# A two-layer adaLN kernel: the expert weight of the first mixture of experts as a square root, spread by DMA

## The chip, the cores and the metric

The kernel runs on one core of one Trainium2 chip. The time is the device time of one execution in microseconds (us). TensorE (PE in the profile) multiplies matrices into the eight banks of PSUM; VectorE (DVE) and ScalarE (ACT) work elementwise on tiles of 128 partitions; SyncE (SP) issues most of the transfers, which run on 16 DMA engines; GpSimd (POOL) is nearly idle here.

## The reference, cut to what matters

Two layers, each of attention and a feed-forward part, over 2048 tokens of width 128. The change is in the first feed-forward part alone, a mixture of 64 experts of which each token uses 8, plus a shared expert:

```
logits = xf @ router_w.T ; scores = sigmoid(logits)
choose 4 of 8 groups, then 8 of 64 experts (by scores + bias)
tw  = scores of the chosen / (their sum + 1e-20) * 2.5          # the combine weight, >= 0
out = sum over experts e:  ( relu(x @ up[e])^2 * tw[:, e] ) @ down[e]     up 128x64, down 64x128
```

Since tw is not negative, relu(u)^2 * tw equals (relu(u) * sqrt(tw))^2.

## The kernel before, in words

Everything is hand-scheduled: each engine has its own program, and semaphores join them. Tokens lie in four chunks of 512 (`NC` = 4). Two experts form a pair, so that one tile has 128 hidden rows; there are 32 pairs, and pair by chunk gives 128 **units**. Weights of four pairs come in one load (`load0`, two slots), which the diff calls slot 0 and slot 1; a loop iteration on every engine has `MU` = 32 units (8 pairs, two loads), and there are four iterations. ScalarE (`high0`) and VectorE (`low0`) split each load into a high and a low fp32r part, in two pieces each, between units; PE waits for these parts (`w0_lo`) before the first unit that uses them.

One unit is, before the change:

- PE, `look0`, three units ahead: three fp32r matmuls (`three`: high by high, high by low, low by high) give the up projection in PSUM bank k % 2; one bf16 matmul with the constant `sel` (a 96-row selector over three bf16 parts of the weights) spreads the combine weights of the pair's two experts over 2 x 64 partitions, in bank 2 + k % 2 (line 839).
- ACT: Relu out of PSUM (`relu0`, L1222), Square (`sq_unit`, L1226), and for three units in four the high fp32r part of the product (`high_unit`, L1231).
- DVE: the product of the spread weight in PSUM and the square (`prod_unit`, L1677), for every fourth unit the high part (L1684), and the fp32r difference (`low_unit`, L1688).
- PE, `sum0`: three fp32r matmuls of the down projection, accumulated in banks 4 to 7.

Ahead of the loop stands the routing on DVE, lines 1580 to 1635, whose last result `b1` (a 128x16x64 tile) is the combine weight; lines 1645 to 1654 split it into three bf16 parts, PE transposes them (L812, L814), and ACT and DVE copy them out of PSUM (L1217, L1704). SP has nothing to issue in the loop but the weight loads (L545, L547). The second layer's mixture of experts already spreads its own weights in the other way: it stores them in DRAM (L618) and reads one row of 2048 back into all 128 partitions (L622).

Of the kernel before, what the change touches and what calls it, by code (L numbers as in the profile page):

```python
# [10 lines left out]
F32 = mybir.dt.float32  # L11
# [6 lines left out]
P = 128  # L18
# [16 lines left out]
EH = E0 // 2  # L35
NCB = 3 * EH
# [67 lines left out]
def adaln_two_layers(nc, A, out):  # L104
    ctx = ExitStack()
    with ctx:
# [105 lines left out]
        comb3 = take([2, NT, 3, EH], BF16)  # L212
        combT = take([2, T], BF16)
        sel = take([NPAIR // 2, P], BF16)
# [4 lines left out]
        relu = take([NBUF, CW])  # L219
        hid = take([2, CW])  # L220
        yT = take([T])
# [53 lines left out]

        cw_dram = nc.dram_tensor("expert_weights", [E1, T], F32).ap()
# [61 lines left out]
        rt_ready = sem("rt_ready")  # L338
        yg_ready = sem("yg_ready")
# [10 lines left out]
        comb_ready = sem("comb_ready")  # L350
        comb_tr = sem("comb_tr")
        comb_T = sem("comb_T")
        comb_TL = sem("comb_TL")
        moe_up = sem("moe_up")
        moe_cb = sem("moe_cb")
        moe_relu = sem("moe_relu")
# [3 lines left out]
        moe_hi_own = sem("moe_hi_own")  # L360
# [81 lines left out]

        def comb_bank(c):
            return 2 - 2 * (c % 2)
# [46 lines left out]
        def _(sp):  # L491
# [73 lines left out]
            sp.dma_start(sel, A["sel"].rearrange("p (n f) -> p n f", f=P)).then_inc(ld_sel, 16)  # L565
# [76 lines left out]
        def _(pool):  # L642
# [9 lines left out]
            pool.wait_ge(vzero, 2)  # L652
            pool.wait_ge(x2_ready, NC)
# [8 lines left out]
        def _(pe):  # L662
# [117 lines left out]
            pe.wait_ge(ld_sel, 48)  # L780
# [22 lines left out]
            pe.wait_ge(ld_c, 16 * 11)  # L803
            for c in range(NC):
                pe.wait_ge(comb_ready, 2)
                if c >= 2:
                    pe.wait_ge(comb_T, c - 1)
                    pe.wait_ge(comb_TL, c - 1)
                b = comb_bank(c)
                pc = ps[:, b:b + 2, :].bitcast(BF16)  # L810
                for k, t in enumerate(tiles(c)):
                    nc.tensor.transpose(pc[0:NCB, 0, k * P:(k + 1) * P],  # L812
                                        comb3[:, 0, t].rearrange("p s e -> p (s e)"), identb[:, :])
                    last = nc.tensor.transpose(pc[0:NCB, 1, k * P:(k + 1) * P],  # L814
                                               comb3[:, 1, t].rearrange("p s e -> p (s e)"), identb[:, :])
                last.then_inc(comb_tr, 1)
            pe.wait_ge(comb_T, NC)
# [1154 lines left out]
```

## Time and profile before

| | us |
|---|---|
| median of 3 runs | 1312.22 |
| the runs | 1310.79, 2832.59, 1312.22 |
| the profiled execution, span from first to last instruction | 1317.5 |
| PE busy | 1166.7 |
| DVE busy | 1046.4 |
| ACT busy | 776.6 |
| bytes read from and written to DRAM | 30.85 MB, 3.08 MB |

For the profiled execution the page gives its span and no other time; the span is 5.3 us above the median. Busy times overlap between engines. Matmuls are pipelined, so a matmul's duration is longer than the distance to the next one. The granted TensorE clock is a share of full speed: 1.00 is 2.4 GHz and 0.50 is 1.2 GHz. The DMA share is the mean busy share of the 16 DMA engines; it is computed from the packets, which may overlap a little, so that a full set of engines reads 0.97 to 1.06.

### The profile page before, as it was taken

Reading aid. Unit: us, or ns where it says so; the run is one execution under the profiler, and the core shown is the slowest. Engines: PE = TensorE matmul, PEld = TensorE weight load, DVE = VectorE, ACT = ScalarE, POOL = GpSimd, SP = SyncE. Lnnn points to the kernel's source line nnn. Section 1 sums busy time; section 2 is a strip of 40 time slices with the busy share of each in tenths; the row PEclk is TensorE's granted clock in tenths of the full one; section 3 lists DMA queues with packets and bytes.
Section 4 is the critical chain, followed back from the end, with each engine's and each line's share of the span. In section 5 each row is a group of like instructions: output and inputs, shape, how many; then the busy total and the mean of one; then the engine's idle time right before and its main releaser. Section 6 shows DMA issues by size and latency. Waiting matters only on the chain.

```text
span 1317.5 us, 17710 instructions
## 1 busy us (share of the span) xinstructions
PE 1166.7 (89%) x6249; PEld 680.9 (52%) x6249; DVE 1046.4 (79%) x2018; ACT 776.6 (59%) x1151; POOL 43.9 (3%) x45
## 2 busy tenths in 40 slices
PE   3888647999999855779999999999998799999998
PEld 2333333666666512345444443443332688888886
DVE  4699998788888883879899889888851688888885
ACT  1635414899999710135555656566676566666664
POOL 0000020000000040140000000000000000000000
PEclk9898767899999956589999999999999699999999
DMA  5000000000000214551000000000000121111001
GB/s 161 0 0 1 0 24 17 16 17 16 18 14 1 78 35 79 72 78 16 2 2 2 1 1 2 1 1 1 1 1 1 45 102 56 56 56 56 0 1 33
DMA packets 38169, 35.02 MB, mean 27 GB/s; under 512 B 15162, under 2 KB 33530, under 8 KB 36810
## 3 DMA queue, kind: packets, MB, share of 16 engines
q1 hardware_dynamic: 36082, 31.12, 9.0%
q0 software_dynamic: 2016, 2.96, 1.7%
q8 instruction: 44, 0.72, 0.2%
q14 instruction: 27, 0.22, 0.1%
HBM read 30.85 MB, written 3.08 MB: 26 GB/s over the span
## 4 chain that ended last, share of the span: by engine, by line
PE 61%; DVE 26%; ACT 6%; issue 3%; DMA 3%; SPq 1%; DVEq 0%; ACTq 0%
PE ps L822 10%; PE ps L823 10%; PE ps L824 10%; PE ps L983 9%; DVE arena_a L1766 7%; PE ps L927 7%; PE ps L971 6%; DVE arena_b L1472 3%; DVE mv L1377 2%; PE ps L839 1%; ACT arena_b L1222 1%; DMA arena_a<-q_parts 1%; PE ps L693 1%; DMA arena_a<-arena_a 1%; DVE xn L1384 1%
## 5 line engine op out<-in xcount | busy, mean ns | idle before, releaser
L1766 DVE TENSOR_REDUCE arena_a<-ps 128x1 f32<-128x512 f32 (+3 forms) x560 | 344.4, 668 | 73.2 <-PE ps L931 46.3
L1289 ACT ACTIVATE arena_b<-ps 128x1024 f32<-128x1024 f32 (+3 forms) x320 | 274.0, 894 | 191.8 <-PE ps L971 169.6
L822 PE MATMUL ps<-parts 128*128 128x512 f32 x640 | 273.2, 427 | 7.1 <-DVE parts L1688 4.2
L823 PE MATMUL ps<-parts 128*128 128x512 f32 x640 | 251.5, 393 | 0.0
L824 PE MATMUL ps<-parts 128*128 128x512 f32 x640 | 251.2, 392 | 0.0
L927 PE MATMUL ps<-arena_b,arena_a 128*128 128x512 bf16 (+3 forms) x576 | 190.4, 354 | 6.3 <-DVE arena_a L1766 4.9
L971 PE MATMUL ps<-arena_a,arena_b 128*128 128x512 bf16 (+3 forms) x576 | 163.2, 348 | 0.7 <-ACT arena_b L1289 0.3
L983 PE MATMUL ps<-arena_b 128*32 128x512 f32 (+3 forms) x1280 | 151.1, 544 | 2.5 <-DVE arena_b L1754 2.2
L822 PEld LDWEIGHTS ps<-parts 128*128 128x128 f32 x640 | 122.0, 191 | 36.8 <-DVE parts L1688 9.7
L824 PEld LDWEIGHTS ps<-parts 128*128 128x128 f32 x640 | 121.0, 189 | 26.4
L823 PEld LDWEIGHTS ps<-parts 128*128 128x128 f32 x640 | 121.4, 190 | 22.4
L1867 DVE TENSOR_TENSOR arena_b<-ps,arena_b 128x512 f32<-128x512 f32 x128 | 88.3, 690 | 55.4 <-PE ps L824 51.6
L927 PEld LDWEIGHTS ps<-arena_b,arena_a 128*128 128x128 bf16 x576 | 52.8, 99 | 143.0 <-DVE arena_a L1766 119.0
L1312 ACT ACTIVATE arena_b<-ps 128x512 f32<-128x512 f32 x128 | 76.6, 599 | 84.5 <-PE ps L824 84.0
L1677 DVE TENSOR_TENSOR arena_b<-ps,arena_b 128x512 f32<-128x512 f32 x128 | 88.1, 689 | 35.2 <-ACT arena_b L1226 34.8
L1688 DVE TENSOR_TENSOR parts<-arena_b,parts 128x512 fp32r<-128x512 f32 x128 | 87.6, 685 | 1.2
L1872 DVE TENSOR_TENSOR parts<-arena_b,parts 128x512 fp32r<-128x512 f32 x128 | 87.3, 682 | 0.1
L1226 ACT ACTIVATE arena_b<-arena_b 128x512 f32<-128x512 f32 x128 | 80.7, 631 | 3.6
L1222 ACT ACTIVATE arena_b<-ps 128x512 f32<-128x512 f32 x128 | 74.9, 585 | 9.2 <-PE ps L824 9.1
L1316 ACT ACTIVATE parts<-arena_b 128x512 fp32r<-128x512 f32 x128 | 79.9, 624 | 0.4 <-DVE arena_b L1867 0.4
L971 PEld LDWEIGHTS ps<-arena_a,arena_b 128*128 128x128 bf16 x576 | 53.3, 99 | 35.0 <-ACT arena_b L1289 13.4
L930 PE MATMUL ps<-arena_b,arena_a 128*128 128x128 bf16 x256 | 53.8, 236 | 12.0 <-DMA arena_a<-q_parts 12.0
(274 smaller groups left out, 1445.3 us busy)
## 6 DMA issues: line engine op xcount, KB each, us to landing
arena_b<-expert_weights SPq DMA_DIRECT2D x7, 1024.0 KB, 6.7
arena_a<-q_parts SPq DMA_DIRECT2D x18, 128.0 KB
arena_a<-q_parts POOLq DMA_DIRECT2D x18, 128.0 KB, 5.9
wslot<-in_L_ffn_up_w SPq DMA_DIRECT2D x8, 256.0 KB, 3.1
wslot<-in_L_ffn_down_w SPq DMA_DIRECT2D x8, 256.0 KB, 3.3
wslot<-in_L_ffn_w_gate SPq DMA_DIRECT2D x8, 256.0 KB, 2.9
wslot<-in_L_ffn_w_up SPq DMA_DIRECT2D x8, 256.0 KB, 3.4
wslot<-in_L_ffn_w_down SPq DMA_DIRECT2D x8, 256.0 KB, 3.8
```

Source lines behind the costliest of these rows:

```text
L822: mm(bank, w(0), x(0), start=start, stop=False)
L823: mm(bank, w(0), x(1), start=False, stop=False)
L824: return mm(bank, w(1), x(0), start=False, stop=stop)
L927: last = mm(b[:, at_:at_ + full], q, kst[:, g, u * CW:u * CW + full], start=True, stop=True)
L971: last = mm(ps[:, 2 + i, full:CW], k, q[:, full:CW], start=True, stop=True)
L983: last = mm(ps[32 * i:32 * i + 32, 6, off:CW], vaug[:, j, g, :], probs[:, s % 2, i, off:CW], start=(j == 0), stop=(j == TPC * c + TPC - 1) ...
L1222: a(relu[:, k % NBUF, :], ps[:, k % 2, :], ACT.Relu).then_inc(moe_relu, 1)
L1289: a(probs[:, s % 2, 2 * pair:2 * pair + 2, off:CW], ps[:, 2 + 2 * pair:4 + 2 * pair, off:CW], ACT.Exp, scale=scale).then_inc(p2_exp, 1)
L1677: v.tensor_tensor(prod0[:, k % NBUF, :], ps[:, 2 + k % 2, :], sq0[:, k % NBUF, :], ALU.mult)\
L1688: v.tensor_tensor(hid0[:, k % NBUF, 1, :], prod0[:, k % NBUF, :], hid0[:, k % NBUF, 0, :].bitcast(F32), ALU.subtract).then_inc(moe_lo, 1)
L1766: v.tensor_reduce(mx[:, n % 2, i:i + fit, t % TPC, u], b[:, 0:fit * w].rearrange("p (h k) -> p h k", k=w), AX_X, ALU.max)\
L1867: v.tensor_tensor(prod1[:, k % NBUF, :], ps[:, 2 + k % 2, :], silg[:, k % 2, :], ALU.mult)\
```

## The change

Three things are changed. First, the routing ends with the square root of the combine weight: ACT takes the root, DVE corrects it by one Newton step, PE transposes the result in fp32 and ACT copies it to `scT` (64 rows by 2048). Second, SP stores `scT` in DRAM (`root_weights`) and loads it back for each pair, spread over the partitions: two rows of 2048, each to 64 partitions, into one of four buffers `cbw`. The spreading matmul goes, with `sel`. Third, the unit is another: DVE forms max(up, 0) * root straight from PSUM, two units ahead; ACT squares that twice, once to fp32 (`sq0`) and once to fp32r (`hid0` high part), and DVE takes the difference of the two. The up projection now has four PSUM banks.

```diff
+            for c in range(NC):
+                sp.wait_ge(comb_T, c + 1)
+                sp.dma_start(sc_dram[:, chunk(c)], scT[0:E0, chunk(c)]).then_inc(st_sc, 16)
+            sp.wait_ge(st_sc, 16 * NC)
+            def load_cb(buf, pair):
+                sp.dma_start(cbw[:, buf, :], sc_dram[bass.ds(2 * pair, 2), :].unsqueeze(1).broadcast_to([2, I0, T]))\
+                  .then_inc(ld_cb[buf], 16)
+            for pair in range(NCBUF):
+                load_cb(pair, pair)
+            for pair in range(NCBUF, 2 * GP):
+                sp.wait_ge(moe_prod, NC * (pair - NCBUF + 1))
+                load_cb(pair % NCBUF, pair)
             with sp.Fori(1, N_IT0) as it:
                 for slot in range(2):
                     sp.wait_ge(w0_lo, it * 4 + (2 * slot - 2))
                     load0(slot, it * 2 + slot)
+                    for k in range(GP):
+                        pair = slot * GP + k
+                        sp.wait_ge(moe_prod, it * MU + NC * (pair - NCBUF + 1))
+                        load_cb(pair % NCBUF, it * (2 * GP) + pair)
...
@@ PE, look0
-                if n0 is not None:
-                    pe.wait_ge(moe_relu, n0 + (k - 1))
-                three(ps[:, k % 2, :], lambda i: up0(slot, i, pair % GP), lambda i: hs0[:, i, chunk(c)],
+                if n0 is None:
+                    pe.wait_ge(comb_T, k + 1)
+                else:
+                    pe.wait_ge(moe_prod, n0 + (k - 3))
+                three(ps[:, k % 4, :], lambda i: up0(slot, i, pair % GP), lambda i: hs0[:, i, chunk(c)],
                       True, True).then_inc(moe_up, 1)
-                w = sel[0:NCB, bass.ds(base + pair % GP, 1), :].rearrange("p a f -> p (a f)")
-                mm(ps[:, 2 + k % 2, :], w, combT[0:NCB, slot, chunk(c)], start=True, stop=True).then_inc(moe_cb, 1)
...
@@ ACT
-            def relu0(n0, k):
...
-            def sq_unit(n0, k):
...
-            def high_unit(n0, k):
+            act.wait_ge(comb_ready, 1)
+            a(b2, b1, ACT.Sqrt).then_inc(rt0_ready, 1)
+                a(scT[0:E0, chunk(c)], ps[0:E0, c, :], ACT.Copy).then_inc(comb_T, 1)
+            def square_unit(n0, k):
                 act.wait_ge(moe_prod, n0 + (k + 1))
-                a(hid0[:, k % NBUF, 0, :], prod0[:, k % NBUF, :], ACT.Copy).then_inc(moe_hi, 1)
+                a(sq0[:, k % NBUF, :], prod0[:, k % NBUF, :], ACT.Square).then_inc(moe_sq, 1)
+                a(hid0[:, k % NBUF, 0, :], prod0[:, k % NBUF, :], ACT.Square).then_inc(moe_hi, 1)
+            def units0(n0, loads, last_iteration):
                 for k in range(MU):
+                    square_unit(n0, k)
                     half, u = k // HALF, k % HALF
                     if u in (4, 6) and not (last_iteration and half):
                         high0((half + 1) % 2, u // 2 - 2, loads * 16 + (32 if half == 0 else 64))
...
@@ DVE
+            dve.wait_ge(rt0_ready, 1)
+            chain(v.tensor_scalar(msk, b2, 1e-18, None, ALU.max))
+            chain(v.reciprocal(sfc, msk))
+            chain(v.scalar_tensor_tensor(sfc, b1, 0.5, sfc, ALU.mult, ALU.mult))
+            v.scalar_tensor_tensor(b1, b2, 0.5, sfc, ALU.mult, ALU.add).then_inc(root_ready, 1)
...
+            def prod_unit(n0, it, k):
+                pair, c = k // NC, k % NC
+                if c == 0:
+                    dve.wait_ge(ld_cb[pair % NCBUF], it * (16 * 2 * GP // NCBUF) + 16 * (pair // NCBUF + 1))
+                dve.wait_ge(moe_up, n0 + (k + 1))
+                v.scalar_tensor_tensor(prod0[:, k % NBUF, :], ps[:, k % 4, :], 0.0, cbw[:, pair % NCBUF, chunk(c)],
+                                       ALU.max, ALU.mult).then_inc(moe_prod, 1)
+            def low_unit(n0, k):
                 dve.wait_ge(moe_sq, n0 + (k + 1))
...
+                dve.wait_ge(moe_hi, n0 + (k + 1))
+                v.tensor_tensor(hid0[:, k % NBUF, 1, :], sq0[:, k % NBUF, :],
                                 hid0[:, k % NBUF, 0, :].bitcast(F32), ALU.subtract).then_inc(moe_lo, 1)
```

How the instructions now stand. First SP's queue from the routing to the end of the loop; in the order `arena_a<-root_weights` is the load of one pair's roots and `wslot<-in_L_ffn_up_w` and `..._down_w` one load of weights. Before:

```order
L562 DMA arena_b<-in_L_ffn_shared_up_w 128x256 [waits x1_ready]
L563 DMA arena_b<-in_L_ffn_shared_down_w 128x2x128
L565 DMA arena_a<-in_sel 128x2048
L567 UNCONDITIONAL_BRANCH
L567 ISA
L545 ISA [waits w0_lo]
L545 DMA wslot<-in_L_ffn_up_w 128x8x64
L547 ISA
L547 DMA wslot<-in_L_ffn_down_w 128x4x128
```

and after the change:

```order
L565 DMA root_weights<-arena_b 64x512 [waits comb_T] x4
L570 DMA arena_a<-root_weights 128x1x2048 [waits st_sc]
L570 DMA arena_a<-root_weights 128x1x2048 x3
L570 DMA arena_a<-root_weights 128x1x2048 [waits moe_prod] x4
L578 UNCONDITIONAL_BRANCH
L578 ISA
L542 ISA [waits w0_lo]
L542 DMA wslot<-in_L_ffn_up_w 128x8x64
L544 ISA
L544 DMA wslot<-in_L_ffn_down_w 128x4x128
L584 ISA
L570 ISA [waits moe_prod]
```

Each load of weights in the loop now stands behind a load of roots that waits for DVE's products, where before it waited for `w0_lo` alone.

Second, ACT just inside the loop. Before, the unit was three instructions with three waits:

```order
L1222 ACTIVATE arena_b<-ps 128x512 [waits moe_up]
L1226 ACTIVATE arena_b<-arena_b 128x512 [waits moe_relu]
L1231 ACTIVATE parts<-arena_b 128x512 [waits moe_prod]
L1221 REGISTER_ALU
L1222 ACTIVATE arena_b<-ps 128x512 [waits moe_up]
```

and after the change it is two with one wait; this stretch is units 4 to 6, where the first piece of a new load of weights (`high0`, L1213) comes between:

```order
L1235 ACTIVATE arena_b<-arena_b 128x512 [waits moe_prod]
L1236 ACTIVATE parts<-arena_b 128x512
L1212 ISA
L1213 ACTIVATE parts<-wslot 128x512 [waits ld_w0_1]
L1234 REGISTER_ALU
L1235 ACTIVATE arena_b<-arena_b 128x512 [waits moe_prod]
L1236 ACTIVATE parts<-arena_b 128x512
```

ACT's squares of unit 5 stand behind its wait for the load of weights, as the Square of unit 5 did before.

## Rows read from the trace of the kernel before

**Rows 1.** Stretches of the loop: length; busy of each engine (instructions); clock; DMA share; GB/s.

```profile
235.00:450.00 215.00, 211.19 (x886) 145.84 (x885) 180.91 (x299) 202.32 (x366) 0.00 (x0) 0.99 0.05 13
300.00:440.00 140.00, 137.58 (x584) 95.62 (x582) 119.03 (x197) 132.24 (x240) 0.00 (x0) 1.00 0.05 11
```

**Rows 2.** Groups by line, 300 to 450: busy, mean ns of one | idle before, releaser.

```profile
L839 PE MATMUL ps<-arena_a 96*128 96x512 bf16 x89 | 34.8, 391 | 0.0
...
L1677 DVE TENSOR_TENSOR arena_b<-ps,arena_b 128x512 f32<-128x512 f32 x90 | 62.0, 689 | 21.9 <-ACT arena_b L1226 21.6
L1688 DVE TENSOR_TENSOR parts<-arena_b,parts 128x512 fp32r<-128x512 f32 x89 | 60.9, 685 | 0.7
L1226 ACT ACTIVATE arena_b<-arena_b 128x512 f32<-128x512 f32 x90 | 56.8, 631 | 2.5
```

**Rows 3.** Timeline, end of the routing to the loop: start, length, engine, line.

```profile
222.93 1.22 DVE L1635 SCALAR_TENSOR_TENSOR arena_a<-arena_a,arena_b 128x1024 f32<-128x1024 f32 x1
...
233.02 0.77 PE L822 MATMUL ps<-parts 128*128 128x512 f32 x1 [0.73 <-DVE arena_a L1704]
...
237.55 1.29 DVE L1677 TENSOR_TENSOR arena_b<-ps,arena_b 128x512 f32<-128x512 f32 x2 [4.80 <-ACT arena_b L1226]
```

**Rows 4.** Groups by line and shape, DVE from 20 to 240, ACT over the span.

```profile
L1486 DVE RECIPROCAL arena_b<-arena_a 128x512 f32<-128x512 f32 x4 | 13.4, 3348 | 2.2 <-ACT arena_a L1157 2.1
L1441 DVE TENSOR_SCALAR arena_b<-arena_a 128x2048 f32<-128x2048 f32 x4 | 4.9, 1228 | 0.1
L1480 DVE SCALAR_TENSOR_TENSOR arena_a<-ps,arena_a 128x512 f32<-128x512 f32 x4 | 2.8, 691 | 0.1
L1477 DVE TENSOR_SCALAR arena_a<-arena_a 128x512 f32<-128x512 f32 x4 | 1.6, 406 | 0.0
```

**Rows 5.** The same view, ACT.

```profile
L1152 ACT ACTIVATE arena_b<-arena_b 128x2048 f32<-128x2048 f32 x8 | 15.3, 1911 | 38.1 <-DVE arena_b L1472 38.1
...
L1214 ACT ACTIVATE arena_b<-arena_b 128x512 f32<-128x512 f32 x8 | 5.0, 630 | 0.3
```

**Rows 6.** Timeline of SP: the store and the first spread load of layer two.

```profile
1046.28 0.30 SPq L618 DMA_DIRECT2D expert_weights<-arena_b  x1
1048.72 0.37 SPq L622 DMA_DIRECT2D arena_b<-expert_weights  x1
```

**Rows 7.** Page, DMA issues: count, KB each, us to landing.

```profile
arena_b<-expert_weights SPq DMA_DIRECT2D x7, 1024.0 KB, 6.7
```

**Rows 8.** Stretches in which loads of 128 rows run (columns as in rows 1).

```profile
10.00:12.00 2.00, 2.00 (x12) 2.00 (x11) 0.00 (x0) 0.00 (x0) 0.00 (x0) 1.00 1.06 400
1056.50:1057.50 1.00, 1.00 (x6) 0.84 (x5) 0.59 (x1) 0.41 (x1) 0.00 (x0) 1.00 0.97 393
1049.80:1058.70 8.90, 8.90 (x39) 7.30 (x39) 6.01 (x10) 6.08 (x11) 0.00 (x0) 0.98 0.90 327
```

**Rows 9.** Stretches in which only loads of 8 rows run (L482, L485).

```profile
514.00:516.00 2.00, 0.00 (x0) 0.00 (x0) 0.00 (x0) 0.00 (x0) 0.00 (x0) 0.50 0.56 62
516.00:518.00 2.00, 0.00 (x0) 0.00 (x0) 0.00 (x0) 0.00 (x0) 0.00 (x0) 0.50 0.58 61
518.00:520.00 2.00, 0.00 (x0) 0.00 (x0) 0.00 (x0) 0.00 (x0) 0.00 (x0) 0.50 0.59 68
```

**Rows 10.** A stretch with one packet, and 20 us with one load of weights.

```profile
273.50:273.82 0.32, 0.32 (x3) 0.25 (x3) 0.20 (x1) 0.32 (x2) 0.00 (x0) 1.00 0.06 26
300.00:320.00 20.00, 19.52 (x84) 13.37 (x83) 16.99 (x29) 18.92 (x35) 0.00 (x0) 1.00 0.10 26
```

**Rows 11.** Timeline, the last unit of the loop.

```profile
449.93 0.69 DVE L1677 TENSOR_TENSOR arena_b<-ps,arena_b 128x512 f32<-128x512 f32 x1 [0.38 <-ACT arena_b L1226]
...
452.90 0.39 PE L824 MATMUL ps<-parts 128*128 128x512 f32 x1
```

**Rows 12.** Page, share of the span on the chain that ended last, by line.

```profile
PE ps L822 10%; PE ps L823 10%; PE ps L824 10%; PE ps L983 9%; DVE arena_a L1766 7%; PE ps L927 7%; PE ps L971 6%; DVE arena_b L1472 3%; DVE mv L1377 2%; PE ps L839 1%; ACT arena_b L1222 1%; DMA arena_a<-q_parts 1%; PE ps L693 1%; DMA arena_a<-arena_a 1%; DVE xn L1384 1%
```

More of the change, by code:

```diff
@@ L34 @@
 NSH = ISH // P
[L35 to L36 removed]
+NCBUF = 4
 LOOK = 3
@@ L210, in adaln_two_layers @@
         b2 = take([NT, E0])
-        comb3 = take([2, NT, 3, EH], BF16)
-        combT = take([2, T], BF16)
-        sel = take([NPAIR // 2, P], BF16)
+        at[0] = PW1 - NCBUF * T
+        cbw = take([NCBUF, T])
         gsm = take([7, NT * NG0])
@@ L218, in adaln_two_layers @@
         wsh = take([2, ISH])
-        relu = take([NBUF, CW])
+        relu = take([2, CW])
         hid = take([2, CW])
+        scT = take([T])
         yT = take([T])
@@ L274, in adaln_two_layers @@
         obuf = take([NT, D])
+        sc_dram = nc.dram_tensor("root_weights", [E0, T], F32).ap()
         cw_dram = nc.dram_tensor("expert_weights", [E1, T], F32).ap()
@@ L350, in adaln_two_layers @@
         comb_ready = sem("comb_ready")
+        root_ready = sem("root_ready")
         comb_tr = sem("comb_tr")
         comb_T = sem("comb_T")
-        comb_TL = sem("comb_TL")
+        st_sc = sem("st_sc")
+        ld_cb = [sem(f"ld_cb{b}") for b in range(NCBUF)]
         moe_up = sem("moe_up")
-        moe_cb = sem("moe_cb")
-        moe_relu = sem("moe_relu")
         moe_sq = sem("moe_sq")
@@ L824, in three, with look0 @@
                 return mm(bank, w(1), x(0), start=False, stop=stop)
-            def look0(base, k, n0, loads):
+            def look0(k, n0, loads):
                 pair, c = k // NC, k % NC
@@ L849, in _ @@
             for k in range(LOOK):
-                look0(0, k, 0 if k >= 2 else None, 2)
-            with pe.Fori(0, N_IT0 - 1) as it:
+                look0(k, None, 2)
+            look0(LOOK, None, 2)
+            sum0(0, 0, False)
+            for k in range(1, MU):
+                if k + LOOK < MU:
+                    look0(k + LOOK, 0, 4)
+                else:
+                    look0(k + LOOK - MU, MU, 6)
+                sum0(0, k, False)
+            with pe.Fori(1, N_IT0 - 1) as it:
                 for k in range(MU):
                     if k + LOOK < MU:
-                        look0(it * GP, k + LOOK, it * MU, it * 4 + 4)
+                        look0(k + LOOK, it * MU, it * 4 + 4)
                     else:
-                        look0(it * GP + GP, k + LOOK - MU, it * MU + MU, it * 4 + 6)
+                        look0(k + LOOK - MU, it * MU + MU, it * 4 + 6)
                     sum0(it * MU, k, False)
@@ L1634, in _ @@
             chain(v.reciprocal(wsum[:, 2, :], wsum[:, 1, :]))
[L1635 to L1654 removed]
+            v.scalar_tensor_tensor(b1, b2, 2.5, wsum[:, 2, :].unsqueeze(2).broadcast_to([P, NT, E0]),
+                                   ALU.mult, ALU.mult).then_inc(comb_ready, 1)
+            dve.wait_ge(rt0_ready, 1)
[3 more added lines that the diff above has]
+            v.scalar_tensor_tensor(b1, b2, 0.5, sfc, ALU.mult, ALU.add).then_inc(root_ready, 1)
             dve.wait_ge(ld_c, 16 * 11)
@@ L1939, in _constants @@
     sin = np.sin(ang).astype(f32).T[d // 2] * np.where(d % 2 == 0, -1.0, 1.0).astype(f32)[:, None]
-    sel = np.zeros((P, NPAIR // 2, P), f32)
-    for n in range(NPAIR // 2):
-        for j in range(2):
-            for m in range(3):
-                sel[m * EH + 2 * n + j, n, j * I0:(j + 1) * I0] = 1.0
     return {
```

99 lines of the change are left out of this document (17 added, 82 removed).

## The prediction, made before the changed kernel was run

> **What bounds the kernel now.** I read the chain of waits first, then the loop's own stretches, then the groups by line, and last the DMA views, since the change moves work from TensorE to the DMA engines. On the chain the matmuls of `three` hold 30% of the span and the spreading matmul 1% [rows 12]. The first layer's loop runs from about 233 to 453 us [rows 3, 11]. In it TensorE is busy 137.58 of 140 us at full clock with 584 matmuls [rows 1], that is 0.236 us for each, and seven to a unit make 1.65 us; ScalarE is busy 132.24 and VectorE 119.03 of the 140 [rows 1]. So TensorE bounds, with ScalarE right behind it: VectorE's idle time of 21.9 us is spent on ScalarE's Square [rows 2]. The DMA engines do almost nothing there: share 0.05, 11 GB/s [rows 1]. Over the whole loop that is 886 recorded matmuls in 215 us [rows 1], or 1.7 us for a unit.
>
> **What the change takes from the unit.** One matmul in seven goes: 0.236 us for each of 128 units, 30 us at most. ScalarE goes from a Relu, a Square and three quarters of a copy to two Squares, of 0.631 us [rows 2] or less: 1.26 us for a unit. VectorE's product becomes one instruction that reads PSUM and a tile; its nearest row, L1480, takes 0.691 us [rows 4], as the old product did with 0.689 [rows 2]; the difference stays at 0.685; the fourth part of a copy goes. So about 1.38 us of VectorE, 1.26 of ScalarE and 6 x 0.236 = 1.42 of TensorE. By compute alone a unit would take 1.42 us, TensorE still ahead. The waits between engines are covered by the two units that VectorE works ahead.
>
> **What it adds to the unit.** The roots now arrive by DMA: each pair needs 1 MiB in `cbw`, 32 MiB in all, more than the whole kernel reads now. A pair's four units take 4 x 1.42 = 5.7 us, so the load must land at 184 GB/s or the loop waits for it. Here lies the decision, and two groups bear on it. Loads with 128 rows keep all 16 engines busy: share 0.97 to 1.06 at 393 and 400 GB/s [rows 8], some 25 GB/s for each engine. Loads whose pattern has only 8 rows outermost, issued by the same SP queue and with many waiting at once, stop at a share of 0.56 to 0.59 [rows 9], half of the full set; 61 to 68 GB/s, since their packets are small. Half the engines for 8 rows means that the engines used are as many as the outermost dimension allows. The new load's source is [2 rows, 64 repeats, 2048 elements]. Its outermost dimension is 2, while the tile written has 128 partitions. The second layer's load, whose source is [128 repeats, 2048], is not like it: it has 128 outermost. If the smaller side decides, two engines carry a pair, 0.5 MiB each.
>
> No row has a load with unlike outer dimensions on its two sides, so the 8-row loads leave open which side counts. The Trainium skill ("DMA: Bandwidth & Descriptors", Why a DMA increments its semaphore by 16 and not by 1) says that a transfer runs on the largest number of engines up to 16 that divides the slowest dimension of both sides; its Rules for kernel authors warn of just such a leading dimension of few copies. By that rule the number here is 2; this trace agrees for 8 and shows nothing for 2 against 128. I take two engines.
>
> **The price of a pair on two engines.** One packet running alone gives 26 GB/s on one engine (share 0.06 is one sixteenth) [rows 10]. With all engines full it is 393/(16 x 0.97) = 25.3 GB/s, and over the second layer's loads 327/(16 x 0.90) = 22.7 [rows 8]. 524,288 bytes on each engine then take 20.2, 20.7 or 23.1 us. I take 20.2, since two engines alone are nearer to the lone packet than to the full set; 23.1 is the upper bound. Below, nothing in the trace is faster. The skill's page gives 27 GiB/s per engine (Specifications); by that alone a pair would take an estimated 18.1 us and the total would be 67 us lower. No run here shows it.
>
> 20.2 us is 3.5 times what the pair's units need, so all of the compute hides behind the loads, and the gain of 30 us is worth nothing.
>
> **The sum, on the profiled execution.**
> - The combine weight is ready at 222.93 + 1.22 = 224.15 us [rows 3].
> - ScalarE's root of 1024 elements: between 0.630 for 512 and 1.911 for 2048 [rows 5], 1.06 us. Its table load (order: ahead of the wait) is hidden in ScalarE's idle time behind the routing.
> - VectorE: maximum, 0.69 us (0.406 for 512, 1.228 for 2048, both in rows 4); reciprocal, twice 3.348 [rows 4] = 6.7; two combining instructions like L1635, 1.22 each [rows 3]. 9.8 us, and about 235.1 us with the root.
> - Sixteen transposes and four copies of about 0.6 us, pipelined as before: 3.3 us, 238.4.
> - Store and wait as in layer two: from the store's issue to the load's, 2.44 us [rows 6]: 241. The first byte some 2 us later: 243. (By now the old loop had begun ten us before, at 233 [rows 3]; the split of lines 1645 to 1654 and its transposes and copies, all on the path, are what it replaces.)
> - 32 pairs one after the other, 32 x 20.2 = 646 us: 889.
> - The six loads of weights inside the loop run through the same two engines: share 0.10 of 20 us [rows 10], 2 us each, 12 us: 901.
> - After the last pair has landed, its four units: the last one from product to last matmul 452.90 + 0.39 - 449.93 = 3.4 us [rows 11], three before it at 1.42 us each, or twice that if TensorE sits at half clock, together 8 to 12 us. I take 9: 910.
>
> The old loop ended at 453.3, so 457 us are added: a span of 1774 us. The median of the runs stood 5.3 us below the profiled span, so **1769 us**.
>
> Two engines must never run dry for this sum. Four buffers allow it: a pair's load is issued when the products of the pair four before are done, so two or three are always queued. The new queue order costs something else: a load of weights stands behind the loads of roots. ScalarE asks for it at units 4 and 6 of each half, and then stands for nearly two pairs, 40 us, with VectorE stopped two or three units later. But in that time two further pairs' loads can be issued and the twelve or so resident units take only 16 to 30 us to catch up. I cost this at nothing; it is covered by the loads themselves. If that cover is gone, each of the six stalls costs up to a pair, 20 us.
>
> TensorE, waiting, should fall to 0.50 granted clock as it does while it waits in rows 9; even at twice 1.42 us a unit, a pair takes 11.4 us and hides. What follows the loop may start at half clock: some us, not counted.
>
> **The rivals.**
> - *All 16 engines carry the load* (the 128 partitions written decide; or the change of DRAM rows is regrouped below the program). For it: the neighbour in layer two lands 1 MiB in 6.7 us [rows 7] beside other loads, and a pair at the full rate, 393 GB/s, takes 2.7 us, inside 5.7. Against it: rows 9. Then the loop gains 30 us, the start loses (241 + 6.7 - 237.55 = 10 us [rows 3, 7]), and a load of weights, issued after the pair-3 products and asked for five units later, may come up to 2 us late six times. Profiled 1297 to 1309, so 1292 to 1304 by the runs, and 1297 in the middle: within 2%, **not slower**. The point from which it decides is 5.7 us for a pair. The skill's rule in the same page's Bandwidth section, at least 1 MiB per DMA for three quarters of the peak, speaks for this one.
> - *Two engines, and the stream breaks at each load of weights*: the stalls above are not covered, six times 20 us: 1889 us. For it: ScalarE's wait stands in front of all its squares. Against: two pairs' loads are released in the stall.
> - *Two engines at the slow rate*, 23.1 us: 93 us more, 1862. It is the upper bound of the likeliest case.
>
> **How the numbers follow.** Two engines with an unbroken stream: 0.81. The broken stream: 0.06. All engines: 0.13. A measurement of this kernel can tell about 2% from no change, that is 26 us, 1286 to 1338. All the slow cases are far above: slower 0.87. Of the third case's 0.13, most lies within 2%; 0.03 falls below 1286, if the starts overlap better: same 0.10, faster 0.03. The range takes in the likeliest case from a few per cent under the lone packet's rate, as the slow-down from neighbours cannot be told from one row (1700), up to the broken stream (1890).
>
> **What would show it.** Right: in the loop a DMA share near 2/16, 0.12 to 0.14, at some 50 GB/s; the landing of a root load near 20 us when alone and up to 80 queued; VectorE's L-line of the new product idle before it for some 450 us, released by the DMA from `root_weights`; stage end near 905; everything else as before. Step by step: 6.7 us for the reciprocal, 0.69 for the new product, two Squares of 0.63. Wrong: a share above 0.3 in the loop and landings under 7 us. The stream is broken if the share drops to 0 between pairs near units 20, 36, 52 and so on.

## The result: 34% slower, and the profile after

| | before | after |
|---|---|---|
| median of the runs, same chip | 1313.01 | 1763.72 |
| the runs | 1310.79, 2832.59, 1312.22, 1313.79 | 1758.29, 1769.85, 1762.44, 1764.99 |
| ratio (95% interval) | | 1.3443 (1.3371 to 1.3515) |
| span of the profiled execution | 1317.5 | 1756.5 |
| first product to end of the first layer's loop | 237.55 to 453.3 | 263.94 to 902.5 |
| PE, DVE, ACT busy | 1166.7, 1046.4, 776.6 | 1187.9, 1038.1, 726.7 |

(Median and span before differ since they are of different executions.) One execution before took 2832.59 us, more than twice the others; nothing on record says why, and the ratio is of the fast executions alone. The prediction was 1769 us. No engine works more than before; the time is idle time. The page of the changed kernel, first the 40 slices (clock, DMA share, GB/s), then the bytes, the chain by line, and the three DMA rows:

```profile
PEclk9898656657575757576675599999999997999999
DMA  4000011111111111111122530000000000221100
GB/s 121 0 1 0 7 36 53 53 62 53 63 53 63 53 62 53 62 58 58 53 99 41 71 71 2 2 1 1 1 1 1 1 1 25 85 72 54 42 1 24
...
HBM read 63.88 MB, written 3.60 MB: 38 GB/s over the span
...
DMA wslot<-in_L_ffn_down_w 9%; SPq L542 7%; PE ps L827 7%; PE ps L994 7%; PE ps L828 6%; PE ps L829 6%; SPq L570 6%; DVE arena_a L1746 5%; DMA arena_a<-root_weights 5%; PE ps L938 5%; PE ps L982 4%; DVE arena_b L1468 2%; DVE mv L1373 1%; DMA arena_a<-q_parts 1%
...
arena_a<-root_weights SPq DMA_DIRECT2D x32, 1024.0 KB
...
wslot<-in_L_ffn_up_w SPq DMA_DIRECT2D x8, 256.0 KB, 33.8
wslot<-in_L_ffn_down_w SPq DMA_DIRECT2D x8, 256.0 KB, 25.9
```

Where the DMA row shows a 1, for fifteen slices, the GB/s row stands at 36 in the first and at 53 to 63 in the other fourteen, and the granted clock falls to 5 to 7 tenths. The chain, which by line was matmuls [rows 12], now has loads and SP's own issue instructions in it. Compare the stretches of the loop with [rows 1] and [rows 8] (same columns):

```profile
243.00:263.00 20.00, 0.00 (x0) 0.00 (x0) 0.00 (x0) 0.00 (x0) 0.00 (x0) 0.61 0.12 51
300.00:440.00 140.00, 52.82 (x168) 38.05 (x168) 37.32 (x59) 32.95 (x58) 0.00 (x0) 0.67 0.14 56
380.00:400.00 20.00, 0.00 (x0) 0.00 (x0) 0.00 (x0) 0.00 (x0) 0.00 (x0) 0.50 0.17 63
```

The first row is the root loads alone, no engine having anything to do: 0.12 is 2/16, at 51 GB/s. In the second, 168 matmuls stand where [rows 1] had 584. In the third all engines have stopped, and the clock is 0.50 (1.2 GHz), but the DMA engines have not: the share is above 2/16 because weights are landing too. The waits from 235 to 910 us (engine, line, what it waited for: us in total, times, longest):

```profile
PE ps L827 <- DVE parts L1670: 418.3, 27, 37.2
ACT arena_b L1235 <- DVE arena_b L1663: 268.8, 86, 25.6
ACT parts L1213 <- DMA wslot<-in_L_ffn_down_w: 240.0, 6, 40.1
DVE parts L1670 <- ACT parts L1236: 218.9, 6, 37.1
DVE arena_b L1663 <- DMA arena_a<-root_weights: 212.0, 20, 28.3
```

Read from the bottom: VectorE's product (L1663) waits 212 us for roots. Six times ScalarE stands some 40 us before the split of the expert weights (L1213), which waits for the load of the down weights, and with it VectorE's difference (L1670) waits, 218.9 us in all; TensorE only passes both on. The timeline at the two ends of the stretch:

```profile
223.84 1.06 ACT L1227 ACTIVATE arena_a<-arena_a 128x1024 f32<-128x1024 f32 x1 [4.88 <-DVE arena_a L1631]
224.93 0.69 DVE L1636 TENSOR_SCALAR arena_a<-arena_a 128x1024 f32<-128x1024 f32 x1 [1.12 <-ACT arena_a L1227]
225.65 6.55 DVE L1637 RECIPROCAL arena_a<-arena_a 128x1024 f32<-128x1024 f32 x1
...
233.50 1.22 DVE L1639 SCALAR_TENSOR_TENSOR arena_a<-arena_a 128x1024 f32<-128x1024 f32 x1
...
236.49 3.03 SPq L565 DMA_DIRECT2D root_weights<-arena_b  x4
241.31 19.46 SPq L570 DMA_DIRECT2D arena_a<-root_weights  x3
...
891.91 0.69 DVE L1663 SCALAR_TENSOR_TENSOR arena_b<-ps,arena_a 128x512 f32<-128x512 f32 x1 [11.61 <-DMA arena_a<-root_weights]
...
902.52 0.69 ACT L1252 ACTIVATE arena_b<-ps,modc 128x512 f32<-128x512 f32 x1 [1.86 <-PE ps L829]
```

From the issue of the first root load (241.31) to the first product on the last one (891.91) are 650.6 us; the last row reads the loop's result.

### The profile page after: what moved, and what is told of

Its sections match the earlier page's. It is cut to its first block, busy times and chain, and to the rows that moved or that the text cites. A ratio compares the mean times of both kernels' runs of the same rounds, so it can differ in the third digit from the quotient of the medians.

```text
span 1756.5 us, 17255 instructions
## 1 busy us (share of the span) xinstructions
PE 1187.9 (68%) x6105; PEld 705.8 (40%) x6105; DVE 1038.1 (59%) x1978; ACT 726.7 (41%) x1056; POOL 43.9 (2%) x45
## 4 chain that ended last, share of the span: by engine, by line
PE 42%; DVE 20%; DMA 16%; SPq 14%; another core or an unknown queue 3%; ACT 2%; issue 2%; DVEq 0%; ACTq 0%
DMA wslot<-in_L_ffn_down_w 9%; SPq L542 7%; PE ps L827 7%; PE ps L994 7%; PE ps L828 6%; PE ps L829 6%; SPq L570 6%; DVE arena_a L1746 5%; DMA arena_a<-root_weights 5%; PE ps L938 5%; PE ps L982 4%; DVE arena_b L1468 2%; DVE mv L1373 1%; DMA arena_a<-q_parts 1%
## 5 line engine op out<-in xcount | busy, mean ns | idle before, releaser
L827 PE MATMUL ps<-parts 128*128 128x512 f32 x640 | 280.8, 439 | 420.6 <-DVE parts L1670 418.3
L827 PEld LDWEIGHTS ps<-parts 128*128 128x128 f32 x640 | 133.9, 209 | 476.4 <-DVE parts L1670 445.7
L828 PE MATMUL ps<-parts 128*128 128x512 f32 x640 | 270.5, 423 | 0.0
L829 PE MATMUL ps<-parts 128*128 128x512 f32 x640 | 268.6, 420 | 0.0
L1663 DVE SCALAR_TENSOR_TENSOR arena_b<-ps,arena_a 128x512 f32<-128x512 f32 x128 | 88.0, 689 | 275.3 <-DMA arena_a<-root_weights 212.0
L1670 DVE TENSOR_TENSOR parts<-arena_b,parts 128x512 fp32r<-128x512 f32 x128 | 87.1, 681 | 219.1 <-ACT parts L1236 218.9
L829 PEld LDWEIGHTS ps<-parts 128*128 128x128 f32 x640 | 132.8, 207 | 31.3
L828 PEld LDWEIGHTS ps<-parts 128*128 128x128 f32 x640 | 134.3, 210 | 26.6
L1847 DVE TENSOR_TENSOR arena_b<-ps,arena_b 128x512 f32<-128x512 f32 x128 | 88.1, 688 | 53.1 <-PE ps L829 47.6
L1308 ACT ACTIVATE arena_b<-ps 128x512 f32<-128x512 f32 x128 | 76.7, 599 | 82.9 <-PE ps L829 82.6
L1213 ACT ACTIVATE parts<-wslot 128x512 fp32r<-128x512 f32 x16 | 9.8, 621 | 240.0 <-DMA wslot<-in_L_ffn_down_w 240.0
L1312 ACT ACTIVATE parts<-arena_b 128x512 fp32r<-128x512 f32 x128 | 79.9, 624 | 0.4 <-DVE arena_b L1847 0.4
L1236 ACT ACTIVATE parts<-arena_b 128x512 fp32r<-128x512 f32 x128 | 78.6, 614 | 0.0
```

The costliest lines, as they stand in the source:

```text
L827: mm(bank, w(0), x(0), start=start, stop=False)
L828: mm(bank, w(0), x(1), start=False, stop=False)
L829: return mm(bank, w(1), x(0), start=False, stop=stop)
L1663: v.scalar_tensor_tensor(prod0[:, k % NBUF, :], ps[:, k % 4, :], 0.0, cbw[:, pair % NCBUF, chunk(c)], ALU.max, ALU.mult).then_inc(moe_prod, 1)
L1847: v.tensor_tensor(prod1[:, k % NBUF, :], ps[:, 2 + k % 2, :], silg[:, k % 2, :], ALU.mult)\
```

## The experiments

Each ratio is to the kernel before, run beside it on the same chip; it is worked out from the single executions, so it can differ a little from the quotient of the two medians. e2, e3 and e5 have one run each, and no ratio. Theory A is the prediction's: the engines that carry a load are as many as the smaller outermost dimension of its two sides, and the loads bound the loop. Rival B: the loads are slow for another reason (the store in DRAM, 64 reads of one row, the queue). Two further questions came up on the way: what a full-rate load would have been worth, and what bounds the new unit then.

**1. How many engines: four, eight, sixteen.** e2_four_rows and e3_eight_rows store the roots two and four times, so that the source has 4 or 8 rows outermost and still writes 128 partitions in one load (`COPIES` = 2 or 4; the stores are left out here):

```diff
-                sp.dma_start(cbw[:, buf, :], sc_dram[bass.ds(2 * pair, 2), :].unsqueeze(1).broadcast_to([2, I0, T]))\
+                rows = sc_dram[bass.ds(2 * pair, 2), :, :].rearrange("e r t -> (e r) t")
+                sp.dma_start(cbw[:, buf, :], rows.unsqueeze(1).broadcast_to([2 * COPIES, I0 // COPIES, T]))\
```

> The changed kernel with every root row stored twice in DRAM and the pair's load written as [4 rows, 32 repeats, 2048]: the same bytes, the same 128 descriptors of 8 KB, the same single instruction for each pair. Theory: 4 engines, 20.27 / 2 = 10.1 us a pair, DMA share 0.25 and about 105 GB/s in the loop; 243 + 324 + 11 = 578, then 854 to 864 us: 1432 to 1442 us. Rival (the 128 partitions written decide, and the slowness has another source, such as the repeats): unchanged, about 1763 us.

> The same with every root row stored four times and [8 rows, 16 repeats, 2048]. Theory: 8 engines, 5.07 us a pair, just under the 5.7 us that a pair's units need, so the loads hide but barely: the loop is bound by TensorE, a load of weights now and then late by a few us; 1295 to 1315 us. Rival as before: about 1763 us.

e1_two_loads makes two loads of a pair's, one row repeated to 64 partitions each, so that 64 is outermost on both sides (VectorE's wait for a pair, not shown, counts both loads):

```diff
-                sp.dma_start(cbw[:, buf, :], sc_dram[bass.ds(2 * pair, 2), :].unsqueeze(1).broadcast_to([2, I0, T]))\
+                for half in range(2):
+                    sp.dma_start(cbw[half * I0:(half + 1) * I0, buf, :],
+                                 sc_dram[bass.ds(2 * pair + half, 1), :].broadcast_to([I0, T]))\
```

> The changed kernel with each pair's load split in two, one row of 2048 repeated to 64 partitions in each, so that the outermost dimension is 64 on both sides; nothing else is changed. Theory (the smaller outermost dimension sets the number of DMA engines): all 16 engines carry it, a pair lands in 3 to 7 us, the DMA share in the loop is about 0.5, and the loop is bound by TensorE at 6 x 0.236 = 1.42 us a unit. Loads from 241, first product 247, loop of 182 us, 4 us of tail, then the 854 to 864 us that follow the loop in the two traces: 1287 to 1297 us, some 1292. Rival (the volume, 32 MiB read from a few hot rows, is slow whatever the shape): it stays above 1700 us.

Measured: e2 1457.09 us and e3 1406.98 us (one run each; before 1311.9), e1 1318.49 us, ratio 1.0036 (0.9996 to 1.0076). The stretches (columns as in rows 1), first e2, twice with the roots alone at its start and then in the loop:

```profile
250.00:255.00 5.00, 0.00 (x0) 0.00 (x0) 0.00 (x0) 0.00 (x0) 0.00 (x0) 0.50 0.25 66
265.00:270.00 5.00, 4.23 (x10) 3.33 (x11) 1.89 (x3) 3.04 (x6) 0.00 (x0) 0.52 0.25 105
300.00:400.00 100.00, 61.77 (x217) 43.99 (x217) 48.81 (x77) 42.58 (x76) 0.00 (x0) 0.78 0.30 112
```

e3:

```profile
300.00:400.00 100.00, 72.04 (x257) 50.73 (x256) 58.51 (x93) 51.28 (x92) 0.00 (x0) 0.83 0.54 144
```

e1, at its start with all loads waiting, and in the steady loop:

```profile
240.00:260.00 20.00, 10.05 (x33) 7.25 (x32) 9.17 (x15) 9.57 (x18) 0.00 (x0) 0.74 0.97 204
340.00:380.00 40.00, 39.69 (x158) 27.71 (x157) 35.56 (x57) 31.74 (x57) 0.00 (x0) 1.00 0.84 186
```

The shares are 2/16 in the changed kernel, 4/16 in e2 with the roots alone and a little more in its loop (weights land there too), a little over 8/16 in e3 and 16/16 in e1. That settles A against B in the number of engines: e1 reads the same DRAM rows through the same queue, writes the same bytes and takes 445 us away. But all three expected times failed: e2 is 15 us above its band, e3 92 us and e1 21 us. In e2 and e3 ScalarE's wait for the down weights stops VectorE's difference as well, for 95.7 and 59.3 us, which the expectations did not have. The bytes per second rise from 53 to 112, 144 and 204: double at the first step, as A has it, and less than that afterwards. 16 engines at 204 GB/s are 12.8 GB/s each, where the lone packet has 26 [rows 10] and the full set of 128-row loads 25 [rows 8]. And e1 is at 1318 us, not below 1300.

**2. Is it the loads that hold e1 up?** e5_floor is e1 with the loads of the first four pairs alone; every later pair uses those roots, so the output is another one.

> The kernel of the two loads a pair, with only the first four pairs' roots loaded; all later pairs reuse them (this leaves 28 of the 32 pairs' weights out of the result). It measures the new unit with no loads beside it. Theory (TensorE bounds the unit): 1.42 us a unit, the same total as with the loads within 3 us, some 1290 us. Rival (the loads that run beside the unit cost it something, late weight loads or a slower VectorE): it is 5 to 15 us faster than the kernel with all the loads.

Measured: 1311.62 us (one run), 6.9 us less than e1; that is inside the rival's 5 to 15 us, and far from the theory's 1290. From 380 to 420 us:

```profile
380.00:420.00 40.00, 39.48 (x157) 27.78 (x156) 35.39 (x57) 31.34 (x56) 0.00 (x0) 1.00 0.00 0
```

There is no DMA traffic at all in this stretch and the pace is that of e1: 157 and 158 matmuls in 40 us, 6 x 40/158 = 1.52 us a unit. So the new unit itself takes 1.52 us, not the 1.42 that the prediction worked out, and the root loads cost e1 only some us. The waits of e1 from 260 to 420 us:

```profile
PEld ps L829 <- DVE parts L1672: 31.8, 77, 5.6
ACT arena_b L1237 <- DVE arena_b L1665: 29.4, 70, 1.4
DVE arena_b L1665 <- PE ps L831: 15.5, 39, 1.2
ACT parts L1215 <- DMA wslot<-in_L_ffn_down_w: 11.1, 6, 6.8
```

TensorE's busy time looks full (39.69 of 40 us in the stretch above), but its matmuls overlap, and 158 in 40 us is not its best pace. Each engine waits for the next for a fraction of a us, some 40 to 80 times in the about 105 units of the stretch: TensorE for VectorE's difference, ScalarE for VectorE's product, VectorE for TensorE's up products. I read that as a ring of waits, which the next experiment tests. TensorE issues the up product of unit k+3 and the down product of k by turns, so the up product stands behind a down product that waits for VectorE.

**3. The ring, the start, the half rate, and the weights: four kernels.** e6_four_ahead is e1 with TensorE four units ahead; since there are four buffers, ScalarE waits for a down product before it overwrites one (the first and the last iteration are changed alike):

```diff
+LOOK0 = 4
...
-                    if k + LOOK < MU:
-                        look0(k + LOOK, it * MU, it * 4 + 4)
+                    if k + LOOK0 < MU:
+                        look0(k + LOOK0, it * MU, it * 4 + 4)
...
+                if k >= NBUF or not first:
+                    act.wait_ge(moe_down, n0 + (k - 3))
                 a(hid0[:, k % NBUF, 0, :], prod0[:, k % NBUF, :], ACT.Square).then_inc(moe_hi, 1)
```

> As e1_two_loads, and TensorE's up products run four units ahead of the down products instead of three (ScalarE waits for the down product before its second squaring, as the buffers stay four). Theory: the unit of 1.52 us in e1_two_loads is a ring of waits (down products, then up products, VectorE's product, ScalarE's two squarings, VectorE's difference, and back), so that one more unit of lead brings the unit to TensorE's six matmuls, 6 x 0.236 = 1.42 us: 128 units x 0.10 = 12 to 13 us less than e1_two_loads, 1305 us (1301 to 1310), with 168 matmuls in 40 us where e1_two_loads had 158. Rival: TensorE's matmul is slower beside the fp32r stores, or VectorE and ScalarE (0.69 + 0.68 and 0.61 + 0.61 us a unit) are the bound by what they lose to each other: then the unit stays 1.52 us and the time at 1318 us.

Measured: 1302.34 us, ratio 0.9913 (0.9875 to 0.9950).

```profile
340.00:380.00 40.00, 39.10 (x169) 31.22 (x168) 36.95 (x60) 32.46 (x59) 0.00 (x0) 1.00 0.96 203
```

169 matmuls for e1's 158: the ring was the bound. But this row also has a DMA share of 0.96 at 203 GB/s: one step later, the half-rate loads are the bound. Four pairs' roots and one load of weights are 4.7 MB, which at 203 GB/s take 23.2 us, 1.45 us for each of 16 units. So the number came as expected, and for the wrong reason: it is not TensorE's limit. Experiment 4 bears this out: with the same lead and full-rate loads the unit is shorter still.

e7_no_newton is e1 without VectorE's four instructions between ScalarE's root and the transposes, which then read ScalarE's result:

```diff
-            dve.wait_ge(rt0_ready, 1)
-            chain(v.tensor_scalar(msk, b2, 1e-18, None, ALU.max))
-            chain(v.reciprocal(sfc, msk))
-            chain(v.scalar_tensor_tensor(sfc, b1, 0.5, sfc, ALU.mult, ALU.mult))
-            v.scalar_tensor_tensor(b1, b2, 0.5, sfc, ALU.mult, ALU.add).then_inc(root_ready, 1)
```

> As e1_two_loads, but ScalarE's square root is used as it is: VectorE's maximum, reciprocal and two scalar-tensor-tensor instructions are left out, so the root is less exact. They took 0.69 + 6.55 + 1.22 + 1.22 = 9.7 us on the path in front of the first root load. Theory: 9.7 us less than e1_two_loads, 1309 us, and the loop begins 9.7 us earlier (first product at 237.8 instead of 247.5 us). Rival: something else is late there (the first expert weights, the last of the residual copies): then 0 to 5 us less.

Measured: 1304.52 us, ratio 0.9912 (0.9876 to 0.9948). In its profile the first product starts at 239.53 us (e1: 247.47), the loop ends at 444.3 (e1: 454.0): 9.7 us sooner, as expected. The ratios differ by 1.2%, 16 us; they are from two chips with intervals of 0.4% each, so that the difference is known to some 7 us either way, and 9.7 us lies just inside. I go by the profile.

e8_interleaved_rows is the changed kernel with the two experts' hidden units interleaved over the partitions, so that one load has a repeat of 64 outermost and covers 128 partitions. The up weights are permuted as they are split, and the down weights loaded interleaved:

```diff
-                sp.dma_start(cbw[:, buf, :], sc_dram[bass.ds(2 * pair, 2), :].unsqueeze(1).broadcast_to([2, I0, T]))\
+                sp.dma_start(cbw[:, buf, :], sc_dram[bass.ds(2 * pair, 2), :].unsqueeze(0).broadcast_to([I0, 2, T]))\
...
+                for j in range(GP):
+                    rows = A["L0_ffn_down_w"][bass.ds(2 * GP * n + 2 * j, 2), :, :].rearrange("two f d -> f two d")
+                    sp.dma_start(wslot[:, slot, (GP + j) * P:(GP + j + 1) * P], rows).then_inc(ld_w0[slot], 16)
```

> The changed kernel with the hidden units of the two experts of a pair interleaved over the partitions (expert 0 on the even ones, expert 1 on the odd ones), so that one load of a pair has an outermost dimension of 64 (a repeat) over 2 rows, and covers all 128 partitions; the up weights are permuted as they are split into high and low parts, the down weights are loaded interleaved. e1_two_loads spread its load over 16 engines too, but each of its two loads wrote 64 partitions, and its packets of 8 KB took 0.58 to 0.60 us at 183 to 204 GB/s. Theory: what slows those is that 64 neighbouring partitions are written at a time; here the packets are back at 0.32 to 0.36 us, full share gives 350 GB/s or more, and the DMA share in the loop is 0.45 to 0.55 instead of 0.84. Rival: the slow packets come from all engines reading the same row (8 KB of DRAM for 64 packets): then 0.58 us and 0.84 again. The time: the unit is 1.52 us in both cases (the loads are not its bound), the weight loads come sooner, so 1308 to 1316 us by the theory, 1316 to 1321 us by the rival.

Measured: 1307.45 us, ratio 0.9937 (0.9901 to 0.9973). First a stretch of e1 at its start, with roots alone:

```profile
245.00:250.00 5.00, 0.00 (x0) 0.00 (x0) 2.44 (x4) 1.80 (x4) 0.00 (x0) 0.50 1.02 215
```

and e8, at its start and in the loop:

```profile
244.00:248.00 4.00, 0.00 (x0) 0.00 (x0) 1.66 (x3) 0.94 (x2) 0.00 (x0) 0.88 1.01 420
...
340.00:380.00 40.00, 39.80 (x158) 27.61 (x157) 34.71 (x56) 31.79 (x57) 0.00 (x0) 1.00 0.61 206
```

With all engines full and roots alone, e8 moves 420 GB/s and e1 215, half of it. In the loop, where weights land too, 206 GB/s at a share of 0.61 are 338 GB/s for a full set, 21 GB/s for each engine; e1 has 186 at 0.84, 221 and 13.8. The rival in the expectation was that all engines read the same row. e8 alone does not exclude it, since its load reads two rows by turns; but the second layer's load reads one row into 128 partitions, and the loads there run at 393 GB/s with a share of 0.97 [rows 8]. So the half rate came neither from reading one row many times nor from the repeat as such, but from writing 64 neighbouring partitions at a time. The share of 0.61 is above the 0.45 to 0.55 that was expected, and the time 0.5 us under its band. The pace is 158 matmuls again, as both theories had it, since the ring is in this kernel too; the wait for down weights is gone (e1's 11.1 us).

The Trainium skill has a rule for this ("SBUF — State Buffer", Door 1: The DMA port swizzle): a transfer's rate depends on how many of 16 ports its partitions reach, and 64 neighbouring ones reach 8, 128 all 16. From its peak of 435 GB/s half is 218, an estimate; the traces agree, with the 215 GB/s of e1 and, for all 128 partitions, the 420 of e8.

e4_no_weight_loads is the changed kernel without the loads of weights inside the loop:

```diff
-                    sp.wait_ge(w0_lo, it * 4 + (2 * slot - 2))
-                    load0(slot, it * 2 + slot)
...
-                        high0((half + 1) % 2, u // 2 - 2, loads * 16 + (32 if half == 0 else 64))
+                        high0((half + 1) % 2, u // 2 - 2, 32)
```

> The changed kernel with the twelve loads of expert weights inside the loop (six pairs of 1024 KB) left out; the first two sets are used throughout, so that the output is wrong. My prediction put 12 us of the stream of root loads down to these six pairs; the trace of the changed kernel leaves about 3 us for them (648.7 us for 32 loads whose 4096 packets of mean 0.315 us on two engines sum to 645). Theory of the prediction: 12 us less than the changed kernel, 1752 us. Reading of the trace: 0 to 4 us less, 1760 to 1764 us, and the span from the issue of the first root load to the end of the last 645 to 649 us. Rival: the six stalls of 40 us of ScalarE on the down weights did hold up the stream after all: then it would be 15 us or more less.

Measured: 1744.66 us (1742.28 to 1747.83), ratio 1.3274 (1.3188 to 1.3360). That is 19 us less than the changed kernel by the medians, which are from two sets of runs. In its timeline the first root load is issued at 240.00 and the first product on the last one is:

```profile
876.00 0.69 DVE L1661 SCALAR_TENSOR_TENSOR arena_b<-ps,arena_a 128x512 f32<-128x512 f32 x1 [11.61 <-DMA arena_a<-root_weights]
```

636.0 us instead of 650.6: the twelve transfers cost 14.6 us, against the prediction's 12. My reading of the trace (0 to 4 us) was wrong: I had taken the mean time of the root packets, which may already hold what the weights' packets between them cost (not tested). The rival, the six stalls of 40 us, asked for 15 us or more: the medians' 19 us would meet it, the profile's 14.6 would not. One load of weights is two transfers of 256 KB, 512 KB together (the expectation has twice that), and what it takes of the engines can be read in e5, in 20 us in which it is the only load:

```profile
310.00:330.00 20.00, 19.81 (x79) 13.77 (x78) 17.59 (x29) 15.44 (x28) 0.00 (x0) 1.00 0.11 26
```

0.11 of 20 us are 2.2 us on each engine, 13 us for the six. So the weights' own packets account for most of the 14.6 us, and the stalls cost 1 or 2 us at most by the profile. Without them VectorE's wait for roots becomes 401.2 us instead of 212.0, and the loop is just as bound.

**4. All together.** e9_exact_root is e8 with TensorE four ahead, as in e6; e9_all_three also leaves out the Newton step, as in e7. Their edits are those above.

> As e9_all_three, with the Newton step kept, so that it computes what the changed kernel computes. Theory: 0.7 to 1.0 per cent above e9_all_three: ratio 0.984 (0.979 to 0.988), near 1296 us, first product near 246 us. Rival: VectorE (0.69 + 0.68 us a unit at 1.42 us) has become the bound of the loop with interleaved rows, and the unit stays near 1.52 us: 0.993.

> e8_interleaved_rows with TensorE four units ahead (as e6_four_ahead) and without the Newton step (as e7_no_newton), so the root is ScalarE's own, a little less exact. Each step's price comes from the earlier runs: e8_interleaved_rows stands at 0.9937 of the kernel before; four ahead took 1.52 us a unit to 1.42 us (0.10 x 128 = 13 us, 1.0 per cent), and the step left out took 9.7 to 14 us (0.7 to 1.1 per cent). Theory, that the three do not overlap: ratio 0.975 (0.970 to 0.980), near 1284 us, loop windows with 168 matmuls in 40 us and a first product near 237 us. Rival: the start's saving is eaten, since the first weights split by ScalarE and TensorE's clock at the loop's start (0.61 to 0.82 granted in its first 20 us) are next in line: 0.983 or more.

Measured: e9_exact_root 1284.48 us, ratio 0.9767 (0.9729 to 0.9805); e9_all_three 1277.00 us, ratio 0.9705 (0.9673 to 0.9736). The first lies below its expected band, the second at its lower edge, and both are faster than the kernel before, by an interval that lies wholly below 1; only e9_all_three's lies wholly more than 2% below. A stretch of e9_exact_root, and its groups by line from 300 to 400 us:

```profile
300.00:400.00 100.00, 100.00 (x443) 82.81 (x442) 97.65 (x158) 88.47 (x157) 0.00 (x0) 1.00 0.63 212
```

```profile
L837 PE MATMUL ps<-parts 128*128 128x512 f32 x148 | 57.6, 389 | 0.0
...
L1676 DVE SCALAR_TENSOR_TENSOR arena_b<-ps,arena_a 128x512 f32<-128x512 f32 x74 | 50.9, 688 | 2.4
L1683 DVE TENSOR_TENSOR parts<-arena_b,parts 128x512 fp32r<-128x512 f32 x74 | 50.5, 683 | 0.0
L1244 ACT ACTIVATE arena_b<-arena_b 128x512 f32<-128x512 f32 x74 | 46.6, 630 | 11.5 <-DVE arena_b L1676 9.9
```

TensorE has no idle time left: 443 matmuls in 100 us, 0.226 us each, 1.35 us for a unit of six. So the 0.236 us of [rows 1], and the prediction's 1.42 from it, are not the floor. VectorE is at 97.65 of 100, and its two instructions take 0.688 + 0.683 = 1.37 us a unit: it is as full as TensorE, and no run separates the two. Where the 0.236 came from is not tested either; in the kernel before, from 300 to 450 us, the first matmul of each three (L822) is recorded longer than the next (L823), and in e9_exact_root all are at 389 ns:

```profile
L822 PE MATMUL ps<-parts 128*128 128x512 f32 x179 | 85.0, 475 | 2.6 <-DVE parts L1688 2.6
L823 PE MATMUL ps<-parts 128*128 128x512 f32 x179 | 70.3, 393 | 0.0
```
From the first product to the loop's end it is 246.49 to 422.9, 176.4 us, where the kernel before took 215.8. So the loop gives 39 us, where one matmul in seven was worth 30 at most; the rest comes with the shorter pace. 9 us of it go back at the start, where the first product comes at 246.49 instead of 237.55.

## Why the prediction was right, step by step

Its mechanism is shown: two engines at 51 to 53 GB/s, a DMA share of 0.12 to 0.13 where the roots run alone, a stream that does not break (in no 10 us from 260 to 890 us is the share below 0.13), and everything else hidden behind it. The terms:

| step | predicted | measured |
|---|---|---|
| end of ScalarE's root and VectorE's correction | 235.1 | 234.7 (233.50 + 1.22) |
| issue of the first root load | 241 | 241.31 |
| one pair on two engines | 20.2 | 19.8 ((636.0 - 2)/32, e4) |
| weight loads inside the loop, together | 12 | 14.6 (e4 against after) |
| last load usable | 901 | 891.9 |
| tail after it | 9 | 10.6 |
| end of the loop | 910 | 902.5 |
| the rest, as before | 864.2 (1317.5 - 453.3) | 854.0 (1756.5 - 902.5) |
| span | 1774 | 1756.5 |

- *The choice between 16 and 2 engines* rested on the 8-row loads of [rows 9]. Four shapes now bear it out, 2, 4, 8 and 64 rows or repeats outermost against 128 or 64 partitions written. The rule of the Trainium skill ("DMA: Bandwidth & Descriptors", Why a DMA increments its semaphore by 16 and not by 1) agrees with all four. By the same page's price for an engine, 27 GiB/s (Specifications), a pair would be an estimated 18.1 us; measured are 19.8, and the rows of the trace were the better source.
- *The pair's time* was 0.4 us too long, 13 us over 32 pairs: the largest miss of the loop, and within what a 26 GB/s printed without decimals can tell (19.8 to 20.6 us). The weight loads took 3 us more.
- *The six stalls at no cost* came as described: 40 us for ScalarE, six times, while the share stayed at 0.13 or more, and e4 leaves 1 or 2 us for them. The sign that VectorE's product would be idle for some 450 us behind the roots came otherwise: it waits 212.0 us for them, and the other 218.9 us stand at the difference, behind ScalarE in the stalls. In e4, without the stalls, the product's wait is 401.2 us.
- *The rest* is 10 us shorter in this execution. The same code after the loop took from 853 (e8) to 865 us (e6) in other profiles, so I take it for scatter between executions; no run shows what makes it.
- *How near 1769 is to 1763.72* is partly luck. The span was forecast 17.5 us too long, 7.5 in the loop and 10 in the rest. The prediction then took off 5.3 us, since the median before stood that far below its profiled span; after the change the median stands 7.2 us above it, and so 12.5 of the 17.5 us cancel.
- *The rival with 16 engines* was priced at 1297 us (1292 to 1304). Its full-rate form, e8, has a ratio of 0.9937, which is 1304 us of the 1312.22 before, the upper edge; e1 is at 1318.49, above it. Two terms of it were off. A unit was to take 6 x 0.236 = 1.42 us since "the waits between engines are covered by the two units that VectorE works ahead": they were not, and it took 1.52 until TensorE ran four ahead, 13 us over 128 units. And a load over 16 engines was put at 393 GB/s without asking which partitions it writes; with 64 it has 204 to 215. Its 10 us at the start were right: 247.47 against 237.55. On the side on which the prediction put it (within 2%) it held.

Not tried: a kernel in which the spreading matmul stays and only the unit's order is changed. So it is open how much of e9's gain the longer lead alone would have given the kernel before.

## What to carry to other kernels

Read a load's outermost dimension on both sides before you trust its size: a repeat belongs outermost, and where two rows go to two halves of the partitions, interleave them. When a load replaces a matmul, work out the time in which it must land from the pace of the unit (5.4 to 6.1 us a pair here). And when the first bound is gone, look for the next: here they were, in order, two engines (1764), the lead of TensorE, 64 partitions at a time, and at last TensorE with VectorE as full beside it (1284, or 1277 with the plain root).

## What the runs showed of the hardware

**SP's issue of a load can block.** The timeline of SP in the changed kernel, first the third of the root loads at the start, then the first load of weights inside the loop:

```profile
242.57 18.20 SPq L570 DMA_DIRECT2D arena_a<-root_weights  x1
...
338.67 20.09 SPq L570 DMA_DIRECT2D arena_a<-root_weights  x1
359.15 19.03 SPq L542 DMA_DIRECT2D wslot<-in_L_ffn_up_w  x1
378.38 5.69 SPq L544 DMA_DIRECT2D wslot<-in_L_ffn_down_w  x1
```

The first two root loads are issued in 0.6 us each, and the third takes 18.20. The two issues of weights take 1.27 and 0.99 us in e1 at first and about 0.4 later; here the first takes 19 us, nearly one pair's time: with several large loads waiting, the next issue seems to go through only when one has landed. That it is the length of the queue that does this is inferred, not tested. It was harmless for the roots. It isn't shown that it lengthens the stalls on the down weights either: the two engines are busy with the roots in front all the time, whenever the issue of the weights ends.

**Rates below the number of engines.** e1's 215 GB/s and e8's 420 agree with the ports of experiment 3. e3 stays unexplained: eight engines, each with 16 neighbouring partitions if they share a load evenly, move 144 GB/s at a share of 0.54, 16.7 GB/s for each, while four engines with 32 partitions each (e2) keep 23 in the loop, and two with 64 keep 26. If all engines stood at the same row of their shares at the same time, the table of ports in the Trainium skill ("SBUF — State Buffer", Door 1: The DMA port swizzle) would put e3 on 4 of them, an estimate of 109 GB/s, and e2 on 2, an estimate of 54. e2 starts near that and leaves it: with its four engines full all the time (share 0.25) it moves 66 GB/s from 250 to 255 us and 105 from 265 to 270. That would fit engines that start in step and drift apart, but what order they keep wasn't measured.
